# A graph network on one core: the second layer of every edge stage one round later, and the first stage's turn from a tile of its own

## The reference

```python
e = _ln(_mlp(edge_feat, edge_enc...)); n = _ln(_mlp(node_feat, node_enc...))
for s in range(2):
    ce = concatenate([e, n[senders], n[receivers]])
    e = e + _ln(_mlp(ce, edge_blk[s]...))
    agg = segment_sum(e, receivers)
    n = n + _ln(_mlp(concatenate([n, agg]), node_blk[s]...))
return _mlp(n, dec...)          # _mlp: silu(x @ w0 + b0) @ w1 + b1; _ln: mean and variance over the 64 channels
```

## Time and profile before

| | |
|---|---|
| median of 3 runs | 15900.21 us (15863.53 to 15902.72) |
| profiled execution | 15783.89 us, span 15782.1 us |
| busy in the span | TensorE 66%, weight loads 48%, VectorE 32%, ScalarE 34%, GpSimd 57% |
| granted TensorE clock, mean | 0.654 of full speed |
| gathers | 3128 in the first stage, 6256 in the other two |

### The profile page before, as it was taken

One profiled execution on the slowest core, in us unless ns is written; L12 is line 12 of the kernel. 1 busy time (PEld: TensorE's weight loads), 2 busy tenths in 40 slices (PEclk: granted clock), 3 DMA queues, 4 the chain that ended last, 5 costly groups with the idle time before them and its releaser, 6 DMA issues. The chain is left out here.

```text
span 15782.1 us, 218306 instructions
## 1 busy us (share of the span) xinstructions
PE 10472.3 (66%) x65479; PEld 7604.9 (48%) x65479; DVE 5063.8 (32%) x10190; ACT 5416.2 (34%) x8544; POOL 8925.4 (57%) x9488
## 2 busy tenths in 40 slices
PE   5677777777777766666666666665666666666666
PEld 4566666666666534343334444443444334444444
DVE  8522222233333322232223333332222222222223
ACT  0233333333333333333333333333333333333333
POOL 1366666666665555555555555555666666666565
PEclk8655555555555566666667677676666676677776
DMA  2111111111111122222223333332222222222222
GB/s 65 23 30 30 30 30 30 30 36 35 36 35 35 39 68 68 70 70 66 68 68 79 78 78 79 77 79 65 55 56 56 55 56 57 59 58 59 58 59 51
DMA packets 1513872, 857.93 MB, mean 54 GB/s; under 512 B 1044173, under 2 KB 1204574, under 8 KB 1512881
## 3 DMA queue, kind: packets, MB, share of 16 engines
q1 hardware_dynamic: 1115074, 571.64, 13.5%
q0 software_dynamic: 302816, 231.81, 9.2%
q10 hardware_dynamic: 95408, 47.86, 1.1%
HBM read 616.95 MB, written 249.33 MB: 55 GB/s over the span
## 5 line engine op out<-in xcount | busy, mean ns | idle before, releaser
L1802 POOL DMA_INDIRECT edge_blk_g<-sender_part,edge_blk_lst x6256 | 5918.2, 946 | 4380.0 <-issue 1810.9
L1402 POOL DMA_INDIRECT fl_gx<-sender_x,fl_lst x3128 | 2958.7, 946 | 2357.2 <-issue 894.1
L1874 ACT ACT_TABLE_LOAD x1564 | 2006.6, 1283 | 60.3 <-ACTq L966 31.9
L1947 DVE SCALAR_TENSOR_TENSOR agg<-edge_blk_aggps,vecs,agg 64x64 f32 x1564 | 441.9, 283 | 4409.4 <-remote 4162.1
L1837 PE MATMUL edge_blk_yps<-b_parts,one_bf 96*128 96x256 bf16 x1564 | 395.6, 346 | 2127.3 <-ACT edge_blk_h L1888 2046.9
L1858 PEld LDWEIGHTS edge_blk_hps<-ident,edge_blk_g 128*128 128x128 f32 x6256 | 1163.5, 251 | 1331.0 <-issue 1315.9
L1880 ACT ACTIVATE edge_blk_sq<-edge_blk_yps 128x512 f32<-128x512 f32 x782 | 466.9, 597 | 3741.4 <-remote 3209.4
L1841 PE MATMUL edge_blk_yps<-w_edge_blk,edge_blk_h 64*128 64x64 f32 x12512 | 1372.7, 368 | 444.6 <-issue 443.6
L1853 PE MATMUL edge_blk_hps<-edge_blk_oha,edge_blk_win 128*128 128x512 f32 x1564 | 1474.2, 1028 | 254.6 <-issue 238.1
L1858 PE MATMUL edge_blk_hps<-ident,edge_blk_g 128*128 128x128 f32 x6256 | 1192.2, 332 | 594.1 <-issue 573.0
L1841 PEld LDWEIGHTS edge_blk_yps<-w_edge_blk,edge_blk_h 64*128 64x128 f32 x12512 | 1215.8, 273 | 638.4 <-issue 637.5
(11 more groups left out here) (278 smaller groups left out, 12248.4 us busy)
## 6 DMA issues: line engine op xcount, KB each, us to landing
edge_blk_e<-edge_state SPq DMA_DIRECT2D x782, 256.0 KB
edge_state<-fl_e SPq DMA_DIRECT2D x391, 256.0 KB
edge_blk_dlb<-local_dst SPq DMA_DIRECT2D x1564, 64.0 KB
edge_blk_g<-sender_part,edge_blk_lst POOLq DMA_INDIRECT x6256
edge_state<-edge_blk_new SPq DMA_DIRECT2D x391, 256.0 KB
fl_gx<-sender_x,fl_lst POOLq DMA_INDIRECT x3128
edge_blk_win<-receiver_part SPq DMA_DIRECT2D x1564, 16.0 KB
fl_attr<-attr_slots SPq DMA_DIRECT2D x391, 32.0 KB
```

What stands on the lines that cost most here:

```text
L1402: pool.indirect_dma_start(out=gx[n.b][:, j % TILES, j // TILES, D:D + X_DIM], out_offset=None, in_=xg_d, in_offset=bass.IndirectOffsetOnAx ...
L1802: pool.indirect_dma_start(out=g[n.b][:, i, 64 * c:64 * c + 64], out_offset=None, in_=ps_d, in_offset=bass.IndirectOffsetOnAxis(ap=lst[n.b] ...
L1874: nc.scalar.activation(idle[:, k:k + 1], eps_c[:, :], func)
```

## The change

In all stages the second layer of a round is one round further back: in the first stage TensorE's body runs `encode(n.back(1))` first and then `second(n.back(3))` (before: `second(n.back(2))` and then `encode`), in the edge stages `second(n.back(2))` (before n-1); ScalarE's `scale` and VectorE's `normed` move with it. `h` gets four buffers in the first stage. In the first stage ScalarE runs `silu` ahead of `scale`. `y_ps` becomes two tiles of one bank, used in turn, and the second layer is 4 matmuls over all 128 rows with the whole `w_mid` in place of 8 over 64 rows. In the first stage VectorE writes the scaled edges twice, into `gx` (for the sums) and into a new tile `t`, which TensorE turns in 4 transposes of 128 columns in place of 8 matmuls with the identity. The dummy activations that load a table write to a place of their own per buffer.

```diff
-        h = many(2, "h", [P, CHUNK])                      # first stage
+        h = many(QUAD, "h", [P, CHUNK])
+        t = many(QUAD, "t", [P, TILES, 2, D])
-        y_ps = ctx.enter_context(nc.psum_tensor("fl_yps", [P, 2, 512], F32))
-        y_all = y_ps[:, :, 0:TILES * D]
+        y_ps = [ps(f"yps{i}") for i in range(2)]
...
-                    wait(pe, t_ok, n.back(1))
-                    for c in range(2):
-                        nc.tensor.matmul(y_ps[:, c, 0:TILES * D], one_bf[:, :], b1_parts[:, 0:TILES * D], start=True, stop=False)
+                    wait(pe, t_ok, n.back(2))
+                    nc.tensor.matmul(y_ps[n.half][:, :], one_bf[:, :], b1_parts, start=True, stop=False)
                     for i in range(TILES):
-                        for c in range(2):
-                            q = slice(64 * c, 64 * c + 64)
-                            ins = nc.tensor.matmul(y_ps[:, c, D * i:D * i + D], h[n.half][q, P * i:P * i + P], w_mid[q, q],
-                                                   start=False, stop=i == TILES - 1)
+                        ins = nc.tensor.matmul(y_ps[n.half][:, P * i:P * i + P], h[n.b][:, P * i:P * i + P], w_mid[:, :],
+                                               start=False, stop=i == TILES - 1)
...
                     for i in range(TILES):
-                        for c in range(2):
-                            ins = nc.tensor.matmul(t_ps[64 * c:64 * c + 64, P * i:P * i + P], gx[n.b][:, i, c, 0:D],
-                                                   ident[:, :], start=True, stop=True)
+                        ins = nc.tensor.transpose(t_ps[:, P * i:P * i + P], t[n.b][:, i, :, :].rearrange("p c d -> p (c d)"),
+                                                  ident[:, :])
...
                 def body(n, i=None, j=None):              # TensorE, first stage
-                    second(n.back(2))
                     encode(n.back(1))
+                    second(n.back(3))
                     turn_in(n)
                     sums(n.back(4))
                     turn(n.back(4))
...
                 def body(n, i=None, j=None):              # ScalarE, first stage
-                    scale(n.back(2))
+                    silu(n.back(1), i, j)
+                    scale(n.back(3))
...
-                    v.tensor_tensor(gx[n.b][:, :, :, 0:D].rearrange("p i c d -> p c i d"), y_all.rearrange("p c (i d) -> p c i d", d=D),
-                                    rs[:, :].rearrange("p (c i d) -> p c i d", c=2, d=1).broadcast_to([P, 2, TILES, D]),
-                                    ALU.mult).then_inc(t_ok, 1)
+                    for to in (t[n.b][:, :, :, :], gx[n.b][:, :, :, 0:D]):
+                        ins = v.tensor_tensor(to, y_ps[n.half][:, :].rearrange("p (i c d) -> p i c d", c=2, d=D),
+                                              rs[:, :].rearrange("p (i c d) -> p i c d", c=2, d=1).broadcast_to([P, TILES, 2, D]), ALU.mult)
+                    ins.then_inc(t_ok, 1)
...
                     one_hots(n.back(2))                   # VectorE, first stage
-                    normed(n.back(2))
+                    normed(n.back(3))
...
                     sums(n.back(3))                       # TensorE, edge stages
                     turn(n.back(3))
-                    second(n.back(1))
+                    second(n.back(2))
...
-                    scale(n.back(1))                      # ScalarE, edge stages
+                    scale(n.back(2))
...
                     finish(n.back(3))                     # VectorE, edge stages
-                    normed(n.back(1))
+                    normed(n.back(2))
```

More of the change, by code:

```diff
@@ L1490, in _ @@
                 pe.wait_ge(s_ld, weights_landed)
-                nc.tensor.matmul(y_ps[:, 0, :][:, 0:NVEC], mean_w[:, :], vecs[:, :], start=True, stop=True).then_inc(s_vm, 1)
+                nc.tensor.matmul(y_ps[0][:, 0:NVEC], mean_w[:, :], vecs[:, :], start=True, stop=True).then_inc(s_vm, 1)
                 pe.wait_ge(s_diag, 1)
                 k = VEC.index("edge_enc")
-                nc.tensor.matmul(y_ps[:, 1, :][:, 0:D], ones_d[:, :], diag[k][:, :], start=True, stop=True).then_inc(s_rows, 1)
+                nc.tensor.matmul(y_ps[1][:, 0:D], ones_d[:, :], diag[k][:, :], start=True, stop=True).then_inc(s_rows, 1)
                 pe.wait_ge(prepared, 1)
                 last = rounds_and_nodes(pe, body, count_sb, 2)
-                second(last.back(2))
                 encode(last.back(1))
+                second(last.back(3))
                 for k in (4, 3, 2, 1):
@@ L1501, in _ @@
                     turn(last.back(k))
-                    if k == 4:
-                        second(last.back(1))
+                    if k > 2:
+                        second(last.back(k - 2))
                 nodes_again(pe, lambda u, j: nodes.pe_whole(pe, u, j), count_sb)
@@ L1536, in body @@
                         nodes.act_late(act, i, j)
-                    silu(n.back(1), i, j)
-                    if i is not None:
                         nodes.act_late_dma(act, i, j)
@@ L1542, in _ @@
                 last = rounds_and_nodes(act, body, count_sb, 2)
-                scale(last.back(2))
                 silu(last.back(1))
-                scale(last.back(1))
+                for k in (3, 2, 1):
+                    scale(last.back(k))
                 wait(act, added, last.back(1))
@@ L1693, in _ @@
                 last = rounds_and_nodes(dve, body, count_sb, 2)
-                for k in (2, 1):
-                    one_hots(last.back(k))
-                    normed(last.back(k))
+                for k in (2, 1, 0):
+                    if k:
+                        one_hots(last.back(k))
+                    normed(last.back(k + 1))
                     add_sums(last.back(k + 2))
                     finish(last.back(k + 2))
-                for k in (2, 1):
-                    add_sums(last.back(k))
-                    finish(last.back(k))
+                add_sums(last.back(1))
+                finish(last.back(1))
                 nodes_again(dve, lambda u, j: nodes.dve_whole(dve, u, j), count_sb)
@@ L1733, in edge_step @@
         red, sd, rs = (sb(k, [P, 8]) for k in ("red", "sd", "rs"))
-        idle = sb("idle", [P, 2])
+        idle = sb("idle", [P, 2 * QUAD])
         h_ps = [ps(f"hps{i}") for i in range(2)]
-        y_ps = ctx.enter_context(nc.psum_tensor(tag + "yps", [P, 2, 512], F32))
-        y_all = y_ps[:, :, 0:TILES * D]
+        y_ps = [ps(f"yps{i}") for i in range(2)]
         t_ps, agg_ps, keys, n_ps = ps("tps"), ps("aggps"), ps("keys"), ps("nps")
@@ L1834, in second @@
                     wait(pe, h_ok, n)
-                    wait(pe, t_ok, n.back(1))
-                    for c in range(2):
-                        nc.tensor.matmul(y_ps[:, c, 0:TILES * D], one_bf[:, :], b1_parts[:, 0:TILES * D], start=True, stop=False)
+                    wait(pe, t_ok, n.back(2))
+                    nc.tensor.matmul(y_ps[n.half][:, :], one_bf[:, :], b1_parts, start=True, stop=False)
                     for i in range(TILES):
-                        for c in range(2):
-                            q = slice(64 * c, 64 * c + 64)
-                            ins = nc.tensor.matmul(y_ps[:, c, D * i:D * i + D], h[n.half][q, P * i:P * i + P], w_mid[q, q],
-                                                   start=False, stop=i == TILES - 1)
+                        ins = nc.tensor.matmul(y_ps[n.half][:, P * i:P * i + P], h[n.half][:, P * i:P * i + P], w_mid[:, :],
+                                               start=False, stop=i == TILES - 1)
                     ins.then_inc(y_ok, 1)
@@ L1866, in _ @@
                     if k == 3:
+                        second(last.back(2))
                         second(last.back(1))
@@ L1904, in _ @@
                 last = rounds_and_nodes(act, body, count_sb, 2)
+                scale(last.back(2))
                 scale(last.back(1))
@@ L1973, in _ @@
                 finish(last.back(3))
+                normed(last.back(2))
                 normed(last.back(1))
```

36 lines of the change are left out of this document (19 added, 17 removed).

## The result

The changed kernel takes 15998.7 us (median of 6 runs, 15956.1 to 16006.9) against 15900.7 us (6 runs of the kernel before on the same chip): a ratio of 1.0062, 95% interval 1.0044 to 1.0081. It is slower by 0.6%; 15,470 us were forecast. The profiled execution has a span of 15,996.6 us, against 15,782.1.

The account below looks back on a forecast made before the run. GpSimd's gathers (10.0 us a round) plus late-counted TensorE completions were taken to bound the kernel. 268 + 167 - 10 = 425 us off 15,783.9 gave 15,359, plus 116 for the median: 15,470 us; own range 15,150 to 15,750, 8-in-10 range 14,900 to 16,500.

Parts of the forecast that it names:

- The step that failed: Second stage: later `pre` gives fewer joined bursts (two rounds' gathers without a pause); 13.3 and 13.2 us a round, 167 us saved.
- fill and drain: Ends of the three stages: one more step at each, some 10 us lost.
- nothing gained, nothing lost: Second layer on TensorE: 8 matmul records of 128 rows replace 16 of 64, 2.0 us against 1.97.
- rival A: Edge stages: the chain `t`, sums, second layer, first layer becomes too long; slower, 16,560 us, chance 0.20.
- First stage: Second layer one round later lets bursts join: 11.57 us a round against 12.48, 268 us saved.
- Rival B: First stage: bursts join but other engines stand still in the second, 14.0 us a round; slower, 16,400 us, chance 0.14.
- Third stage: Longer path to `pre` still fits before the release; stays at 12.3 to 12.5 us a round, no gain.
- Turn: First stage, TensorE: 4 real transposes replace 16 records, 1.12 us against 1.98, not on GpSimd's wait.
- Second scaling 0.69: First stage, VectorE: writing both `t` and `gx` adds 0.69 us a round; cost zero, 270 us at most.
- a change of mode: TensorE: the weight load behind the bias matmuls waits 0.41 us, linked to a tiling-mode change; that pause should go.
- The base of the argument: All stages: TensorE completions in a burst's first 5 us count at once, later ones some 1.7 us after its end.
- 10.0 us a round in all is excluded as long as GpSimd must wait once in two rounds: All stages: lower limit stated with the much-faster rival (14,480 us, chance 0.11); gathers alone take 10.0 us a round.

Follow-up runs that it names:

- e7: Kernel before with only the edge stages' second-layer form changed (128-row matmuls, two output tiles, later wait for `t`, separate `idle` places): 16,229 us, ratio 1.020.
- e9: Kernel before with the edge stages' new second-layer form, two output tiles and separate `idle` places, but the old wait for `t`: 16,028 us, ratio 1.018.
- e6: Kernel before with the edge stages' second layer moved one round back, old matmul form, separate `idle` places: 16,173 us, ratio 1.017 to the kernel before.
- e3: Changed kernel with SyncE issuing the next round's list ahead of the edge load that waits for `new`: 15,310 us, ratio 0.962 to the kernel before.
- e5: Changed kernel with GpSimd in the edge stages waiting for `pre` of three rounds back instead of four: 15,278 us, ratio 0.961 to the kernel before.
- e1: Kernel before with only the first stage's part of the change, edge stages as before: 15,679 us, ratio 0.986.
- e12: Changed kernel with the list ahead, plus GpSimd waiting in edge stages for a round's first four gathers to land: 14,870 us, 0.945 to the kernel before.
- e14: Changed kernel with four more two-column matmuls ahead of each edge-stage second layer, on the fourth chip: 12,406 us, ratio 1.000 to the kernel before.

## Why the prediction was wrong

**The step that failed** is "In the second stage the later `pre` makes it rarer that a completion falls in the first 5 us, so there are fewer joined bursts", a term of -167 us. The stage took +363 us. The forecast of the profiled execution was 15,359 us, and its span came out at 15,996.6: of these 638 us, 530 are this step's, 94 the first stage's, 24 the third's, less 10 of fill and drain that were allowed for. (The 116 us by which the median of before exceeds its profiled run were added to the forecast and have no counterpart in the changed kernel, so the medians differ by 529.) `pre` came earlier within a joined burst (4.0 for 4.9 us), there were 166 joined bursts for 109, and each pair costs 29.5 us for two rounds where two single bursts cost some 25. A second term failed with it, "nothing gained, nothing lost" for the matmuls of the second layer: their duration was right, but that form (with its two output tiles and the `idle` tile) costs 2.0% by itself (e7) and 1.8% with the old wait (e9), and brings the 166 and 168 joined bursts. The delay alone (e6) does make `pre` later in single bursts, as I had said (8.4 for 7.3 us), but joined bursts get no rarer (113), and it costs 1.7%, in part as rival A has it, by GpSimd's wait for `pre`. I had added up the chain behind the release (`t`, sums, second layer, first layer) and asked only what the delay does to it.

**What joined bursts cost** was on the page: the earlier trace rows have 30.9 us for two rounds and name the late list. I used it as a rate and did not ask why the list is late. e3 and e5 show it: SyncE's list stands behind a load that waits for `new`. Each of the two edits takes some 700 us off the changed kernel, and with the list ahead the edge stages of both kernels take nearly the same time.

**First stage**: right in mechanism, too large by a third. The bursts do join, as foreseen (two rounds in three by the forecast, 64% of the rounds by the count). A pair costs 20.0 + 3.7 = 23.7 us and not 22.4. With that, (23.7 + 12.3) / 3 = 12.0 us a round, which is what rows of the result show; 174 us were gained, 268 forecast. e1 confirms it alone (0.986). Rival B fell: VectorE stands, but the list does not come late behind it.

**Third stage**: nothing, as forecast (+24 us); rival A's longer chain is seen as a wait of the sums for `t` (2594.5 us of idle time before L1814 over both edge stages, by the page), but it does not reach GpSimd.

**The durations on TensorE and VectorE** were right. Second layer 2.0 us: it takes 1.92 us for 8 records at the low clock. Turn: 1.06 us in 4 records at 3045.17. Second scaling 0.69: two instructions of 0.69 and 0.68 us at 3056.51 and 3057.12. The Trainium skill (TensorEngine Tiling (Array Packing), Theoretical Speedup) would have the halves of 64 rows side by side run up to twice as fast; 1.97 us before and 1.92 after for the same work do not show it here. The idle time before the second layer's weight loads, which the prediction put down to a change of mode, fell from 638.4 to 142.3 us over the edge stages.

**The base of the argument**, that a completion in the first 5 us of a burst counts and a later one doesn't, is seen on three chips for `pre` in plain bursts and isn't a law. In e12 `pre` counts at once 8 us into a row, and in e5 sums are held that end 2 to 3 us into one. "10.0 us a round in all is excluded as long as GpSimd must wait once in two rounds" fell on the fourth chip. There the changed kernel itself wasn't run; e14, which is that kernel with more matmuls still, has a ratio of 1.000. Why one chip holds completions back and another doesn't was not found. Nor was it settled why the new form of the second layer, equal in duration, joins the bursts; the runs made for that landed where nothing is held.

**The range**: its upper end, 15,750 us, was said to be half of each term, which gives 15,690. It doesn't matter beside a miss of 529.

## What to carry to other kernels

When a page says that the bounding engine waits for a small load, look at what stands ahead of that load in its queue: here a list of 16 values a partition stood behind a load that waited for VectorE, and moving it was worth 2.6% in the one kernel and 4.4% in the other, where the change itself moved 0.6%. When an engine can run ahead, ask what its head start does to the others; here two rounds of gathers without a pause cost more than they gave, and stopping them earlier was faster. And before a tuning is kept that trades on the pace of completions, time it on more than one chip: the wait amid the gathers, put into the edge stages, was worth 1.8% by the ratios of e12 and e3 (the same kernel without it), and put into all stages it cost 20% on a chip that holds nothing back.

## What the runs showed of the hardware

- On three chips, while GpSimd issues indirect DMAs 1.25 us apart without a pause, many completions of the other engines are taken up only after the last one: in the second stage of the kernel before, VectorE starts again 2.2 us after a burst of eight and 3.2 us after a joined one, in the median, after standing still for 18 us in the joined one. TensorE's own matmul records with landed operands come one in about 2 us (idle 1.77 and 1.75 us before L1851). Not all are held: in e12 `pre` is taken up 0.04 us after it ends, 8.3 us into a row. On the fourth chip, same program and same spacing, the delay is 0.03 us. The Trainium skill (SBUF — State Buffer, SBUF: two separate sides) says of the engine side that "only the shared port pair causes contention" and that TensorE and ScalarE never wait on anyone there; these waits are then of another kind than that page's, and no run here shows which.
- In e12 a pause of GpSimd of 2.2 us was enough for the sums that had been held back to be counted, though it stands in the middle of a round.
- The kernel before took 12,405 us on one chip of four and 15,732 to 15,908 us on the others, 22% and 1% apart. Whether that lies in the chip or in something else about that machine isn't shown.
